# Four transformer blocks on one core: the causal attention's plan and transfer order, its last output, and the feed-forward's weight splits are rearranged

## The reference, cut to what matters

```python
x = x + attn_a(layernorm(x), Wqkv, Wo)           # causal, ALiBi, 32 heads of 16, one shared K and V
x = x + ffn(layernorm(x), c1_w, c2_w, w1, w2t)
x = x + attn_b(layernorm(x), wq, wk, wv, wo)     # 32 heads of 128, window 128, rope
x = x + ffn(layernorm(x), c1_w, c2_w, w1, w2t)   # the same weights

# attn_a
scores = einsum('bqhd,bkd->bhqk', q, k) * scale + slope_h * (pos_k - pos_q), masked where k > q
out = softmax(scores) @ v ; return out @ Wo
# ffn: in each of 56 groups of 32 hidden units only the one with the largest router score works
inter = x @ c1_w.T @ c2_w.T                      # 1792 scores per token
h = relu(x @ w1[idx].T) ; out = h @ w2t[idx]     # idx: the first maximum of each group of 32
```

## Time and profile before

| | |
|---|---|
| median of 3 runs | 3085.81 us (3084.63 to 3087.61) |
| the profiled execution, its own time | 3086.43 us |
| its span in the trace | 3084.6 us |
| PE, DVE, ACT, POOL busy | 87%, 67%, 36%, 32% of the span |
| causal attention | 0 to 592 us |
| first feed-forward; second | from 593 us; 2611 us to the end |
| mean granted clock of PE | 0.936 of full speed |

### The profile page before, as it was taken

One profiled execution on the slowest core, in us unless ns is written; L12 is line 12 of the kernel. 1 busy time (PEld: TensorE's weight loads), 2 busy tenths in 40 slices (PEclk: granted clock), 3 DMA queues, 4 the chain that ended last, 5 costly groups with the idle time before them and its releaser, 6 DMA issues. The chain is left out here.

```text
span 3084.6 us, 41728 instructions
## 1 busy us (share of the span) xinstructions
PE 2678.1 (87%) x14452; PEld 2053.9 (67%) x14452; DVE 2074.2 (67%) x4129; ACT 1121.8 (36%) x2436; POOL 976.9 (32%) x716
## 2 busy tenths in 40 slices
PE   3879898567989979999999987999999998589899
PEld 2444454255767757888888865788888886467677
DVE  2745645255777577778778757777877875657766
ACT  1345345222122244444444434444444443221221
POOL 1112011134222234444444423444444441342222
PEclk7799899778999999999999999999999999789999
DMA  5133332400000011110101100111010101100000
GB/s 189 31 107 84 81 106 59 140 1 0 1 0 0 23 35 35 35 34 27 32 9 34 34 29 8 35 35 34 27 32 8 34 21 44 63 1 15 14 14 14
DMA packets 112462, 117.64 MB, mean 38 GB/s; under 512 B 7028, under 2 KB 83956, under 8 KB 112308
## 3 DMA queue, kind: packets, MB, share of 16 engines
q1 hardware_dynamic: 112340, 116.04, 12.4%
HBM read 93.21 MB, written 22.81 MB: 38 GB/s over the span
## 5 line engine op out<-in xcount | busy, mean ns | idle before, releaser
L1762 POOL TENSOR_TENSOR rope_straight<-rope_straight,rope_crossed 128x512 f32<-128x512 f32 x160 | 206.8, 1292 | 478.4 <-DVE rope_crossed L1571 478.4
L520 POOL TENSOR_TENSOR f_hidden_low<-f_hidden,f_hidden_high 128x512 fp32r<-128x512 f32 x112 | 144.3, 1288 | 603.0 <-ACT f_hidden_high L468 603.0
L1667 ACT ACTIVATE probs<-probs,exp_bias 128x256 f32<-128x256 f32 (+1 forms) x512 | 240.7, 471 | 167.9 <-DVE exp_bias L1553 167.5
L896 DVE TENSOR_REDUCE a_max<-a_work 128x1 f32<-128x384 f32 (+3 forms) x352 | 209.6, 637 | 115.6 <-PE a_work L787 108.2
L261 PE MATMUL f_hidden_sum<-f_z_high,f_w_high 128*128 128x512 f32 x448 | 195.4, 436 | 75.7 <-POOL f_w_low L539 64.3
L1001 ACT ACTIVATE a_probs<-a_scores 128x512 f32<-128x512 f32 x320 | 173.0, 599 | 172.8 <-PE a_scores L801 95.9
L1412 PE MATMUL proj<-y_high,wq_high 128*128 128x512 f32 x512 | 213.3, 417 | 18.4 <-DVE y_low L1541 12.0
L782 PE MATMUL a_work<-a_keys,a_queries 64*128 64x256 f32 (+3 forms) x512 | 148.9, 443 | 71.9 <-DMA a_queries<-a_q_stacked 40.4
L1412 PE MATMUL w_sum<-o_high,wo_high 128*128 128x512 f32 x512 | 203.8, 398 | 7.6 <-DVE xt L1595 4.7
L372 DVE SCALAR_TENSOR_TENSOR f_hidden<-f_hidden_sum,f_mask_turned 128x512 f32<-128x512 f32 x112 | 77.0, 687 | 189.3 <-ACT f_mask_turned L463 172.2
L1412 PE MATMUL proj<-y_low,wq_high 128*128 128x512 f32 x512 | 204.0, 398 | 0.0
(11 more groups left out here) (239 smaller groups left out, 7683.8 us busy)
## 6 DMA issues: line engine op xcount, KB each, us to landing
a_queries<-a_q_stacked SPq DMA_DIRECT2D x16, 1024.0 KB, 6.3
wq_raw<-in_L_attn_b_wq SPq DMA_DIRECT2D x32, 512.0 KB
wo_raw<-in_L_attn_b_wo SPq DMA_DIRECT2D x16, 1024.0 KB, 6.8
a_q_stacked<-a_q_part_high SPq DMA_DIRECT2D x32, 256.0 KB
f_w_raw<-in_L_ffn_w SPq DMA_DIRECT2D x14, 512.0 KB, 10.1
f_w_raw<-in_L_ffn_w2t SPq DMA_DIRECT2D x14, 512.0 KB, 10.9
xt<-n_L_attn_a_hidden_states SPq DMA_DIRECT2D x4, 1024.0 KB, 29.3
a_q_stacked<-a_q_part_low SPq DMA_DIRECT2D x16, 256.0 KB
```

What stands on the lines that cost most here:

```text
L520: e.tensor_tensor(hl[:, j % 2], hm[:, :], f32(hh[:, j % 2]), ALU.subtract).then_inc(hl_ready, 1)
L896: e.tensor_reduce(mx[:, t % 2, to:to + nh], bank, AX.X, ALU.max).then_inc(work_free[k], 1)
L1667: e.activation(part, part, ACT.Exp, bias=bias[:, n % 2, t:t + 1], scale=SM_SCALE, accum_out=total[:, n % 2, t:t + 1]).then_inc(exp_done, 1)
L1762: e.tensor_tensor(ra[:, slot], ra[:, slot], rb[:, slot], ALU.add).then_inc(roped, 1)
```

## The change

**Causal attention, plan.** The pairs of maxima are spread over all 20 slots, two or three in each, and the ten first pairs of the next batch's tile 2 are made in slots 16 to 19. Batch 0 has its own table, since its tile 1 leaves the prologue. `KV` and `Q` come eight slots earlier, `Wo` up to three. The LayerNorm sums are made for the batch after next, in slots 12 and 15, and those of batch 1 in the prologue. ACT's, DVE's and POOL's steps of LayerNorm and output move with them (`high_out` from units p = 16 to 19 to 12 to 15, `invert_sums` from p = 8 to 6; two units make a slot).

**Transfers.** SP's prologue loads `ones`, then `x` of batch 0 in four parts, the key rows, `Wqkv`; the other batches' `x` and `Wo` come later, between other steps. In each batch SP's order is new. DVE makes two of the four low z of batch 0.

**Last output.** For the last batch the sums go from the output tile straight into the SBUF tile `sums`; columns 0 to 383 (`EARLY`) are inverted, loaded, split and multiplied (`WoA`) before the rest; only the last 128 columns remain for the tail. ACT issues half of the last store.

**Feed-forward.** `high_w1` and `low_w1` run two chunks ahead instead of one. Before the first batch ACT makes the squares before `c1h`, POOL instead of DVE makes the low parts of `c1` and `c2` (and then `low_w1(0)`, `low_w1(1)`, `low_w2(0)`), z is normalised in four pieces, and the router's first product follows piece by piece.

```diff
+        SEARCH = {0: (2, 2), 1: (2, 2), 2: (2, 2), 3: (3, 3), 4: (3, 2), 5: (3, 2), 6: (3, 3), 7: (3, 2), 8: (3, 2),
+                  9: (3, 2), 10: (4, 2), 11: (4, 2), 12: (5, 2), 13: (5, 2), 14: (5, 2), 15: (5, 2), 16: (6, 2),
+                  17: (6, 3), 18: (6, 2), 19: (6, 3)}
+        SEARCH_FIRST = SEARCH | {0: (1, 4), 1: (1, 4)} | {s: (2, 4) for s in range(2, 6)} | {s: (3, 4) for s in range(6, 10)}
+        OPENS = {3: ("mT", 2), 4: ("Vt", 0), 10: ("mT", 3), 13: ("mT", 4), 17: ("mT", 5)}
+        CLOSES = {0: ("KV", 0), 2: ("Q", 0), 3: ("Q", 1), 5: ("Q", 2), 7: ("Q", 3), 9: ("Wo", 0), 11: ("Wo", 1),
+                  12: ("mean", 0), 13: ("Wo", 2), 14: ("Wo", 3), 15: ("var", 0)}
...
+            yield "small", "mean", 1, 0
+            yield "small", "var", 1, 0
+            for i in range(MAX_PAIRS[0]):
+                yield "max", 0, 0, i
+            yield "small", "mT", 0, 0
...
+                    if b == 0 and s in (1, 5):
+                        yield "small", "mT", 0, 1 if s == 1 else 2
...
+            for d in range(DT):
+                yield "small", "WoA", NB - 1, d
...
+                    if b == NB - 1 and p == 28:
+                        e.wait_ge(o_stored[0], 16 * OUT_DMAS * 2 * NB)
+                        e.wait_ge(o_stored[1], 16 * OUT_DMAS * (2 * NB - 1))
+                        e.reciprocal(sums[0:96, :], sums[0:96, :]).then_inc(inv_ready, 1)
...
# SP, the loop over batches, as it is after
                if b:
                    for half in range(2):
                        store_out(e, b - 1, 3, half)
                    load_sums(b - 1)
                if more:
                    send_keys(b + 1)
                if b == 0:
                    send_max(0, 1)
                if b == NB - 1:
                    store_inverses(b - 1)
                for half in range(2):
                    store_out(e, b, 0, half)
                if 0 < b < NB - 1:
                    store_inverses(b - 1)
                if more:
                    send_queries(b + 1, 0)
                if b:
                    send_max(b, 2)
                if more:
                    send_queries(b + 1, 1)
                if b == 0:
                    send_max(0, 2)
                for m in range(DT) if b else ():
                    load_out(b - 1, m)
                if more:
                    send_queries(b + 1, 2)
                for half in range(2):
                    store_out(e, b, 1, half)
                if more:
                    send_queries(b + 1, 3)
                    queries_stored(b + 1)
                    load_queries(b + 1, 0)
                    load_queries(b + 1, 1)
                send_max(b, 3)
...
# ffn, ACT and POOL, first batch
                     if first and c + 1 < NCH:
-                        low_w1(c + 1)
+                        if c + 2 < NCH:
+                            low_w1(c + 2)
                         low_w2(c + 1)
...
+            e.wait_ge(c_high, 1)
+            e.tensor_tensor(c1l[:, :, :], c1_raw[:, :, :], f32(c1h[:, :, :]), ALU.subtract).then_inc(c_low, 1)
+            e.wait_ge(c_high, 2)
+            e.wait_ge(c_low, 1)
+            rest = slice(64, CROWS)
+            e.tensor_tensor(c2s[rest, :], c2_raw[rest, :], f32(c2s[rest, :]), ALU.subtract).then_inc(c_low, 1)
+            e.wait_ge(c_low, 2)
             low_w1(0)
+            low_w1(1)
             low_w2(0)
...
+            def first_router():
+                bank, full = aux_write(e, None, "T")
+                e.wait_ge(c_low, 1)
+                for d in range(DT):
+                    e.wait_ge(zh_ready, d + 1)
+                    e.matmul(bank[0:CROWS, :], c1h[:, d, :], zh[:, d, :], start=d == 0, stop=False)
+                    e.matmul(bank[0:CROWS, :], c1l[:, d, :], zh[:, d, :], start=False, stop=False)
+                    e.wait_ge(zl_ready, d + 1)
+                    mm = e.matmul(bank[0:CROWS, :], c1h[:, d, :], zl[:, d, :], start=False, stop=d == DT - 1)
```

More of the change, by code:

```diff
@@ L495, in _ @@
             high_t(None)
+            high_w1(1)
             high_w2(0)
@@ L559 @@
 OUT_DMAS = 11
+EARLY = S - P
 def pair_of(p):
@@ L648, in of_batch, with searches @@
                 return (kind, b + i // ST, i % ST) if b + i // ST < NB else None
-            return (kind, b + 1, i) if b + 1 < NB else None
-        def searches(b, s, part):
-            if s not in SEARCH:
-                return
-            t, n = SEARCH[s]
-            if b + t // ST >= NB:
-                return
-            done = sum(k for r, (u, k) in SEARCH.items() if u == t and r < s)
-            for i in range(n * part // 4, n * (part + 1) // 4):
-                yield "max", b + t // ST, t % ST, done + i
-        def plan():
+            ahead = 2 if kind in ("mean", "var") else 1
+            return (kind, b + ahead, i) if b + ahead < NB else None
+        def plan():
+            done = {}
+            def searches(b, s, part):
+                t, n = (SEARCH if b else SEARCH_FIRST).get(s, (0, 0))
+                tile = b + t // ST, t % ST
+                if tile[0] < NB:
+                    for _ in range(n * part // 4, n * (part + 1) // 4):
+                        done[tile] = done.get(tile, 0) + 1
+                        yield "max", *tile, done[tile] - 1
             yield "small", "mean", 0, 0
@@ L764, in small @@
                     e.wait_ge(wo_low, 1)
+                    cols = slice(0, EARLY) if kind == "WoA" else slice(0, S)
                     for m in range(DT):
[L766 to L767 removed]
+                        mm = three(bank[:, cols], [x[:, m, i * P:(i + 1) * P] for x in (woh, wol)],
+                                   [x[:, m, cols] for x in (ath, atl)], m == 0, m == DT - 1)
                 mm.then_inc(full, 1)
@@ L833, in _ @@
                     weigh(*step)
-            tail = [*(x[:, :] for x in work), sbank[0][:, :]]
+            tail = [x[:, 0:P] for x in (*work, sbank[0])]
             for k, bank in enumerate(work):
@@ L881, in small @@
                     e.sem_inc(free, 1)
-                elif kind == "Wo":
+                elif kind in ("Wo", "WoA"):
                     e.wait_ge(full, n)
-                    here = xt[:, i, b * S:(b + 1) * S]
-                    e.tensor_tensor(here, here, bank[:, :], ALU.add).then_inc(free, 1)
+                    n = S if kind == "Wo" else EARLY
+                    here = xt[:, i, b * S:b * S + n]
+                    e.tensor_tensor(here, here, bank[:, 0:n], ALU.add).then_inc(free, 1)
             def find_max(b, t, i):
@@ L1046, in _ @@
                     copy_out(*step)
+            store_out(e, NB - 1, 3, 1)
+            for m in range(DT):
+                high_out(NB - 1, m, slice(0, EARLY))
             for m in range(DT):
@@ L1241, in _ @@
                     load_queries(b + 1, 1)
-                store_out(b, 2)
+                send_max(b, 3)
+                if b == 0:
+                    load_x(3)
                 if more:
                     load_queries(b + 1, 2)
+                for half in range(2):
+                    store_out(e, b, 2, half)
+                if more:
                     send_max(b + 1, 0)
```

306 lines of the change are left out of this document (172 added, 134 removed).

## The result

The changed kernel takes 2996.09 us, the median of four runs (2992.69 to 2998.08); the ratio to the kernel before is 0.9706, 95% interval 0.9689 to 0.9723. That is 90 us less, half of the 180 forecast, and outside the range. The profiled execution spans 2994.9 us against 3084.6.

The account below looks back on a forecast made before the run. PE, busy 87% of the span, was taken as the bound, so time could come only from its waits and low clock. Gains of 77 + 12 + 10 + 20 + 32 + 12 + 17 = 180 us gave 2906 us, range 2862 to 2968.

Parts of the forecast that it names:

- Weights two chunks ahead: Feed-forwards: low weights made a chunk earlier end PE's wait for POOL; six intervals fall from 115.5 to 77 us, gain 77.
- Rival 3: Feed-forwards: the wait moves to another low part in POOL's queue, 77 us lost, 2983 us; chance 0.03.
- Start of the feed-forward: Before each feed-forward's first batch: earlier squares, c2 off DVE and z in pieces gain 6 us, twice, 12 in all.
- Rival 1: Feed-forward chunks: POOL's weight subtractions lock out DVE, making chunks 14.2 us, above PE's 12.3; 2935 us, chance 0.15.
- Prologue: Attention's prologue: keys go some 9 us earlier, first maxima at 62 or 63 us; gain 10 us, bounds 5 and 14.
- Batch 0: Attention's first batch, from the turn of tile 0 to its end: 140 us falls to 120, gain 20, bounds 32 and 8.
- Batches 1 and 2: Attention's middle batches: PE's floor 95 to 101 us plus waits and clock makes 108 each; gain 16 each, 32 in all.
- Batch 3: Attention's last batch: 73 us of PE work less ten pairs made ahead, plus 4, makes 72; gain 12 us.
- Last output: Attention's tail: 33.9 us falls to 17, with the early product hidden in the transfers; gain 17 us, bounds 20 and 8.
- rival 2: Attention: SP's in-order queue delivers queries late, PE stands and its clock falls; 40 us lost, 2946 us, chance 0.18.
- Rival 4: Attention: ACT's earlier high_out stands for POOL's out tiles, stopping exponentials and PE; kernel slower, 3100 us at 65 per batch, chance 0.04.
- The signs: Trace marks if right: chunks 12 to 13 us, maxima near 62, clock above 0.95, a_max waits below 10, tail some 18.

Follow-up runs that it names:

- second run of the changed kernel: The changed kernel run again unedited, as the measure for runs on the same chip: 2992.99 us, ratio 0.9699 to the kernel before.
- The version with all the edits: Changed kernel plus last output's order, LayerNorm sums in slots 10 and 12, tile 1 in prologue, later high parts, earlier Q, batch 0's even maxima, feed-forward start: 2936.84 us.

## Why the prediction was wrong, point by point

- **Weights two chunks ahead, 77 us: right.** Six intervals fell from 117.2 and 115.6 to 75.7 and 79.1, 78 us in all; no wait for a low weight is left. Rival 3 is out.
- **Start of the feed-forward, 12 us: about 3.5.** The first mask copy comes 39.3 and 39.1 us after the table load instead of 42.3 and 39.6. The step had seen that POOL's subtractions would run beside DVE's chain and took off 2; it should have priced the rest of a POOL subtraction in each link, 1.8 and 2.0 us over 0.69, in each of the two feed-forwards. The run with c2 back on DVE gets 3.3 and 5.4 us more, which with the 3.5 is the forecast's 12, or a little less for the spread of the second. Rival 1's mechanism was right here, but in the chunks it did not decide: intervals of 12.6 and 13.2, not 14.2. The argument against it misread its row: POOL's w2 began at 665.78, when w1 ended, and not with the end of L365 at 666.37.
- **Prologue, 10 us: 4.7.** The keys go at 36.75, 6.9 us earlier and not 9, the queries' load at 60.67 instead of 67.20, and the first maxima begin at 67.58 instead of 73.16, not at 62 or 63.
- **Batch 0, 20 us: a loss of 8.4, the largest miss.** The failed term is the low clock, and beside it DVE. The step took 98 us of PE work and 22 for waits and clock. The windows give 124.4 us busy, of which some 25 are the price of the low clock (66% of 17.33 and 36% of 107.09, halved), so the work is 99, as forecast. But the clock takes 25 where 5 were allowed, though the step's own rows had shown 21 of it before (114.8 busy, 94 at full clock) and none showed why it should go. PE stands 24 us: 9.3 for the rows of maxima, where 11 were allowed, 0.2 for queries, where 4 were, 11.1 for DVE's reductions and 4.0 for DVE's other work. The step had said that slots 0 to 9 run at DVE's pace, but added nothing for it to PE's 98. The step had counted two pressures, sends and DVE's pace, one at a time, and none for LayerNorm in slots 12 to 19. Tile 1 in the prologue gives 12 us back and LayerNorm elsewhere 8.
- **Batches 1 and 2, 16 us each: 16.9 in batch 2, none in batch 1** in the first pair of traces, some 16 and 6 by the means. In batch 1 three terms were too small. The clock takes 11.8 us in the first trace and 7.3 in the second (22% of 107.33 and 14% of 103.93, halved), where 3 were allowed. LayerNorm meeting the maxima was given 4 and took 9 to 12 (from the third output copy to the last, 305.4 to 350.4, batch 1 takes 45.0 us, batch 2 33.0; in the second run of the changed kernel 41.6 and 33.0). ACT's exponentials hold PE 4.1 us, for which the sum had nothing. The 4 us for queries were right (5.1 and 4.5). That batch 2's number came out is partly luck: the gain was put down to the even stream of maxima, and that alone was worth 6.4 us.
- **Batch 3, 12 us: 5.3.** Its PE work is 67.7 us by the same reckoning, as forecast (68.5); it stands 9 us, 6.9 of them for ACT's exponentials, where the sum had 4 in all. The high parts are one reason, but with them moved the batch was no shorter.
- **Last output, 17 us: a loss of 3.2.** The sum of links was sound, since the run with the order mended has a tail of 21.6 us against the 18.7 that the forecast comes to (35.7 - 17). What failed is the sentence that the early product hides in the transfers, and its price "up to 8 if late". ACT's copies stand behind its last stores and DVE's reciprocal behind the early adds, and that cost 17.
- **The rivals.** Transfers (rival 2) hold PE 24 us in the attention, below its mark of 40. Rival 4's wait is there, 13.3 us on ACT, and with the high parts moved PE's wait for exponentials fell from 16.1 to 4.3 us; other waits took a part of that back.
- **The signs.** Those of the feed-forwards came. Those of the attention did not: besides the first maxima, the clock was 0.89 and 0.95 in batches 1 and 2 and not above 0.95 in both, the reductions held PE 12.8 us and not under 10, and the tail was 38.9 us and not some 18.

The miss is not one rival. The last output, LayerNorm and the high parts were each moved beside something else and priced without what stood ahead of them in an in-order queue, or beside them on DVE; and in batches 0 and 1 the low clock, which the rows of before had shown, was forecast to go with nothing to show why.

## What to carry to other kernels

Where a change puts work "early so that it hides", write down for each engine what stands ahead of it and behind it in that engine's own order; two steps moved within the order of ACT and DVE here were worth 17 us. Where two streams are spread evenly, lay the other periodic work on the same table before pricing a slot: LayerNorm in slots 12 to 19 cost batch 1 9 to 12 us, and 3 to 10 of them came back when its first product stood where PE waited for a transfer. Don't let a wait or a low clock that the rows show fall out of the sum unless a row shows what ends it. The version with all the edits takes 0.9503 of the kernel before (0.9485 to 0.9521), against 0.9706 for the change alone.

## What the runs showed of the hardware

- PE with products in its prologue stand keeps a granted clock of 1.00 (2.4 GHz) from 50 to 60 us, where it was 0.61 without them; in the first maxima, which begin at 68 us, it is at 0.50 (1.2 GHz) from 75 to 90 either way. Filling a stand of 12 us brought batch 0's end 0.5 us forward.
- DVE's SCALAR_TENSOR_TENSOR with both tensor inputs in SBUF is held by POOL as its TENSOR_TENSOR is: 2.52 and 2.71 us beside POOL's subtractions, 0.69 without them.
- The untouched window attention took between 1543 and 1554 us in different kernels, and batch 1 of the same schedule between 116.0 and 122.9 us in four traces. Both spreads are larger than several of the gains told here; the marks within a trace narrow them, and for batch 1 even they need more than one trace.
